# PSUM banks given by expected release in place of a ring, and the engines' orders within a substep arranged anew, in a macaron block (windowed attention, state-space scan, windowed attention)

## The reference, cut to what matters

```python
def attn_layer(x, Wqkv, qs, ksc, Wo):          # 16 heads of 64
    q, k, v = split(x @ Wqkv)                  # x with half of its features shifted by a token
    q = l2norm(q) * qs; k = l2norm(k) * ksc
    q = q * cos * scale + rotate_half(q) * sin * scale
    k = k * cos * inv + rotate_half(k) * sin * inv
    # windows of 32 queries against 64 keys, masked, softmax of 8*q.k, times v
    return local_attention(q, k, v) @ Wo

def ffn_layer(x, g, bln, W1, b1, W2, b2):
    xn = layernorm(x) * g + bln
    a, gate = split(xn @ W1 + b1)              # 341 + 341
    return a * gelu(gate) @ W2 + b2

for i in range(6):
    x = attn_layer(shift_tokens(x), ...) + x
    x = ffn_layer(shift_tokens(x), ...) + x
```

## Time and profile before

| | |
|---|---|
| median of 3 runs | 3372.07 us (3358.28 to 3372.07) |
| the profiled execution's own time | 3364.97 us |
| its span, first to last instruction | 3363.2 us |
| mean granted TensorE clock | 0.946 of full speed |
| VectorE (DVE) busy | 2933.3 us, 87% |
| TensorE (PE) busy | 2891.1 us, 86% |
| GpSimd (POOL) busy | 2423.5 us, 72% |
| ScalarE (ACT) busy | 2059.8 us, 61% |

### The profile page before, as it was taken

One profiled execution on the slowest core, in us unless ns is written; L12 is line 12 of the kernel. 1 busy time (PEld: TensorE's weight loads), 2 busy tenths in 40 slices (PEclk: granted clock), 3 DMA queues, 4 the chain that ended last, 5 costly groups with the idle time before them and its releaser, 6 DMA issues. The chain is left out here.

```text
span 3363.2 us, 132089 instructions
## 1 busy us (share of the span) xinstructions
PE 2891.1 (86%) x57914; PEld 1829.9 (54%) x57914; DVE 2933.3 (87%) x4224; ACT 2059.8 (61%) x3820; POOL 2423.5 (72%) x1679
## 2 busy tenths in 40 slices
PE   5689988988999989897677788999998989998987
PEld 3455555655666655553233455555565555555553
DVE  6789989999999988986898789889899989898984
ACT  3466666666676666665663566666566666566663
POOL 3678787787787787874464678778787787787773
PEclk8899999999999999998897899999999999999998
DMA  5233333333333333320002233333343333342330
GB/s 136 65 80 77 82 91 74 84 92 71 84 92 73 89 85 72 88 65 28 10 4 59 68 81 78 75 93 77 73 101 73 86 90 71 82 94 65 88 74 15
DMA packets 114726, 250.85 MB, mean 75 GB/s; under 512 B 27244, under 2 KB 60648, under 8 KB 114152
## 3 DMA queue, kind: packets, MB, share of 16 engines
q1 hardware_dynamic: 114152, 242.40, 30.5%
HBM read 37.82 MB, written 3.15 MB: 12 GB/s over the span
## 5 line engine op out<-in xcount | busy, mean ns | idle before, releaser
L1096 ACT ACTIVATE squares<-general 128x512 f32<-128x512 f32 x768 | 453.7, 597 | 716.8 <-PE general L661 707.8
L1290 POOL TENSOR_TENSOR probs<-probs,row_sum 128x1024 f32<-128x1024 f32 x192 | 365.4, 1903 | 442.4 <-DVE row_sum L968 442.3
L1270 POOL TENSOR_TENSOR q_ring<-q_ring,partner 128x512 f32<-128x512 f32 x384 | 491.0, 1279 | 203.9 <-DMA partner<-sines 203.3
L881 DVE TENSOR_TENSOR sines<-general,layer_tables 128x512 f32<-128x512 f32 x768 | 515.8, 672 | 85.3 <-ACT squares L1096 81.8
L1270 POOL TENSOR_TENSOR k_ring<-k_ring,partner 128x512 f32<-128x512 f32 x384 | 490.9, 1278 | 0.0
L695 PE MATMUL general<-probs_t,v_buf 32*64 32x64 f32 x24576 | 339.0, 234 | 153.8 <-issue 85.1
L659 PE MATMUL general<-xs_hi,wqkv_lo 128*128 128x512 f32 x768 | 454.2, 591 | 18.5 <-DVE xs_lo L908 8.0
L695 PEld LDWEIGHTS general<-probs_t,v_buf 32*64 32x64 f32 x24576 | 304.0, 134 | 246.1 <-issue 237.5
L1284 POOL TENSOR_TENSOR probs<-probs,q_scale 128x1024 f32<-128x1024 f32 x192 | 365.4, 1903 | 15.1
L722 PE MATMUL general<-k_ring,q_ring 64*32 64x64 f32 (+1 forms) x24576 | 295.3, 223 | 92.5 <-issue 53.1
L671 PE MATMUL general<-att,wo 128*128 128x512 f32 x768 | 366.2, 621 | 4.6 <-ACT att L1166 4.2
(11 more groups left out here) (233 smaller groups left out, 6369.9 us busy)
## 6 DMA issues: line engine op xcount, KB each, us to landing
partner<-sines SPq DMA_DIRECT2D x1536, 128.0 KB, 2.3
wqkv_raw<-in_wqkv SPq DMA_DIRECT2D x80, 208.0 KB, 2.7
wo<-in_wo SPq DMA_DIRECT2D x12, 512.0 KB, 5.1
w<-in_w SPq DMA_DIRECT2D x12, 341.0 KB, 3.2
base_dram<-x SPq DMA_DIRECT2D x8, 256.0 KB, 2.4
att<-in_wqkv SPq DMA_DIRECT2D x2, 1024.0 KB, 6.7
sines<-base_dram SPq DMA_DIRECT2D x8, 256.0 KB, 3.9
w<-in_w SPq DMA_DIRECT2D x12, 128.0 KB
```

The source lines that it names most:

```text
L881: e.tensor_tensor(by_seq(sines[:, i % 2, which, :]), g, both(layer_tables[:, 2 * which + 1, :]), ALU.mult).then_inc(S[f"sin_{side}"], 1)
L1096: e.activation(squares[:, (2 * p + which) % 4, :], general_of(("proj", k, n, p, which))[:, :], ACT.Square).then_inc(S[f"squared_{side}"], 1)
L1270: e.tensor_tensor(y, y, partner[:, i % 2, which, :], ALU.add).then_inc(S[f"rotated_{side}"], 1)
L1290: e.tensor_tensor(y, y, spread_keys(row_sum[:, i % 2, :]), ALU.mult).then_inc(S["probs_done"], 1)
```

## The change

It replaces the ring by a choice: each product takes the bank with the smallest expected release time, `until`, counted in substeps from HOLD; among equals the next in ring order. The walk follows the new order of TensorE. And it moves parts of a substep on TensorE, VectorE and GpSimd. Several names are split (gates and gelus, values_of and hidden and so on), with the same lags as before; on ScalarE the lines change places only among parts that never fall in the same substep, so that its order stays.

```diff
+HOLD = {"proj0": 0.35, "proj1": 0.7, "spread": 0.65, "scores": 0.5, "var": 0.7, "center": 1.1, "gate": 0.6, "value": 0.5, "ffn_out": 0.8, "att": 1, "v": 1, "project0": 1.1, "project1": 1.1}
@@ class Banks
     def around(self, banks):
         self.banks, self.next, self.written = banks, 0, {}
+        self.step, self.until = 0, {}
     def use(self, key, sem, value):
         at = self.next
+        if self.banks == POOL_BANKS:
+            at = min(range(self.banks), key=lambda i: (self.until.get(i, 0), (i - self.next) % self.banks))
         self.next = (at + 1) % self.banks
+        name = f"{key[0]}{key[-1]}" if key[0] in ("proj", "project") else key[0]
+        self.until[at] = self.step + HOLD.get(name, 1)
@@ Banks.stack
-            g = k * ITEMS
+            g, self.step = k * ITEMS, st.t
@@ tensor_stack (Banks.stack in the same order)
                 proj 0, spread
-                if st.out_first:
-                    pe_out(e, w, k, *st.out_first)
                 scores, var
+                if st.out_last is not None:
+                    pe_out(e, w, k, st.out_last, 1)
                 center
+                if st.out_first is not None:
+                    pe_out(e, w, k, st.out_first, 0)
                 ffn_out
-                if st.gates is not None:
-                    pe_gates(e, w, k, st.gates)
                 values_of
-                if st.enter:
-                    pe_enter(e, w, k, *st.enter)
                 proj 1, attention products
-                if st.out_last is not None:
-                    pe_out(e, w, k, st.out_last, 1)
+                if st.gates is not None:
+                    pe_gates(e, w, k, st.gates)
+                if st.enter:
+                    pe_enter(e, w, k, *st.enter)
                 v
@@ vector_stack
                 rotate q, scale the scores, var, last output added
+                if st.first_added is not None:
+                    dve_out(e, w, k, st.first_added, 0)
                 hidden, norms back, first splits
-                if st.split is not None:
-                    dve_split_tokens(e, w, k, st.split)
+                if st.turn:
+                    dve_turn(e, w, k, *st.turn)
                 ffn added
-                if st.out_first:
-                    dve_out(e, w, k, *st.out_first)
                 root, enter
+                if st.split is not None:
+                    dve_split_tokens(e, w, k, st.split)
                 rotate k
-                if st.turn:
-                    dve_turn(e, w, k, *st.turn)
                 norms, sums
-                if st.v:
-                    dve_v(e, w, k, *st.v)
                 sum_inv, max
+                if st.v:
+                    dve_v(e, w, k, *st.v)
@@ gpsimd_stack
                 subtract, scale and affine, scale the scores
-                if st.center is not None:
-                    pool_square(e, w, ("ffn", k, st.center))
                 if st.load_split:
                     pool_split_pair(e, w, k, *st.load_split)
+                if st.enter:
+                    pool_enter(e, w, k, *st.enter)
+                if st.center is not None:
+                    pool_square(e, w, ("ffn", k, st.center))
                 if st.added:
                     pool_rotate(e, w, k, *st.added, 0)
-                if st.exps:
-                    pool_probs(e, w, k, *st.exps)
-                if st.enter:
-                    pool_enter(e, w, k, *st.enter)
                 if st.added:
                     pool_rotate(e, w, k, *st.added, 1)
+                if st.probs:
+                    pool_probs(e, w, k, *st.probs)
```

More of the change, by code:

```diff
@@ L108, in __init__ @@
         self.exps = self.group(t, EXP_LAG)
+        self.probs = self.group(t, PROBS_LAG)
         self.turn = self.group(t, TURN_LAG)
@@ L120, in __init__ @@
         self.spread = self.group(t, SPREAD_LAG)
-        self.out_first = next(((self.item(t, at), i) for i, at in ((0, 17),) if self.item(t, at) is not None), None)
+        self.out_first = self.item(t, 17)
+        self.first_added = self.item(t, 17)
         self.out_last = self.item(t, 21)
+        self.last_added = self.item(t, 21)
+        self.shift = self.item(t, 21)
         self.center = self.item(t, 22)
         self.var = self.item(t, 23)
+        self.var_turn = self.item(t, 23)
         self.root = self.item(t, 24)
         self.gates = self.item(t, 25)
+        self.gelus = self.item(t, 25)
         self.values_of = next(((self.item(t, at), js) for at, js in ((26, (0,)), (27, (1, 2))) if self.item(t, at) is not None), None)
+        self.hidden = next(((self.item(t, at), js) for at, js in ((26, (0,)), (27, (1, 2))) if self.item(t, at) is not None), None)
         self.ffn_out = self.item(t, 28)
+        self.ffn_added = self.item(t, 28)
+        self.ffn_shift = self.item(t, 28)
         self.load = (n // CHUNKS + 1, p) if self.now and n % CHUNKS == CHUNKS - 1 and n // CHUNKS + 1 < DEPTH else None
@@ L287, in stack @@
                 self.var(("ffn", k, st.var))
+            if st.out_last is not None:
+                self.use(("project", k, st.out_last, 1), "att_added", (g + st.out_last) * 2 + 2)
             if st.center is not None:
                 self.norm(("ffn", k, st.center))
+            if st.out_first is not None:
+                self.use(("project", k, st.out_first, 0), "att_added", (g + st.out_first) * 2 + 1)
             if st.ffn_out is not None:
                 self.use(("ffn_out", k, st.ffn_out), "ffn_added", g + st.ffn_out + 1)
-            if st.gates is not None:
-                for j in range(len(HIDDEN_CUTS)):
-                    self.use(("gate", k, st.gates, j), "gelu_done", (g + st.gates) * 3 + j + 1)
             if st.values_of:
@@ L309, in stack @@
                     self.use(("att", k, n, group, j), "att_kept", ((g + n) * GROUPS + group) * 4 + j + 1)
-            if st.out_last is not None:
-                self.use(("project", k, st.out_last, 1), "att_added", (g + st.out_last) * 2 + 2)
+            if st.gates is not None:
+                for j in range(len(HIDDEN_CUTS)):
+                    self.use(("gate", k, st.gates, j), "gelu_done", (g + st.gates) * 3 + j + 1)
+            if st.enter and st.enter[1] == 0:
+                self.norm(("enter", k, st.enter[0]))
+            if st.enter and st.enter[1] == 1:
+                self.var(("enter", k, st.enter[0]))
             if st.v:
@@ L509, in macaron_kernel @@
             for st in PLAN:
-                for key in (("att", k, st.out_last), ("ffn", k, st.ffn_out), ("enter", k, st.enter[0] if st.enter and st.enter[1] == 2 else None)):
+                for key in (("att", k, st.shift), ("ffn", k, st.ffn_shift), ("enter", k, st.enter[0] if st.enter and st.enter[1] == 2 else None)):
                     if key[2] is not None and key[2] not in (range(ITEMS - CHUNKS, ITEMS) if key[0] == "ffn" else ()):
@@ L1194, in scalar_stack @@
                     act_k_inv(e, w, k, *st.spread)
+                if st.split is not None:
+                    act_split_tokens(e, w, k, st.split)
+                if st.center is not None:
+                    act_center(e, w, ("ffn", k, st.center))
                 if st.norms_back is not None:
                     act_norms(e, w, k, st.norms_back)
[L1197 to L1202 removed]
+                if st.gelus is not None:
+                    act_gelus(e, w, k, st.gelus)
                 if st.now:
@@ L1224, in scalar_stack @@
                     act_enter(e, w, k, *st.enter)
-                if st.ffn_out is not None and st.ffn_out < ITEMS - CHUNKS:
-                    n = st.ffn_out
+                if st.ffn_shift is not None and st.ffn_shift < ITEMS - CHUNKS:
+                    n = st.ffn_shift
                     w.wait_ge(S["ffn_added"], k * ITEMS + n + 1)
```

64 lines of the change are left out of this document (27 added, 37 removed).

## The result

The changed kernel takes 3436.53 us (median of four: 3433.2, 3435.01, 3438.04 and a disturbed execution of 4283.97, which the ratio leaves out) against 3371.48: ratio 1.0199, 95% interval 1.0167 to 1.0231. It is slower by 65 us where 3383 was forecast; the time lies inside the range of 3310 to 3440, near its upper end.

The account below looks back on a forecast made before the run. A loop: VectorE bounds p6's second rotation to p2's scores, TensorE p2's attention products to p6's proj 1. Terms 34 + 4 + 9 - 6 - 9 + 10 - 10 - 16 + 2 = +18 us on 3365.0: 3383, range 3310 to 3440.

Parts of the forecast that it names:

- slower by over 0.5%: Case that the kernel takes above 3389 us: both slower rivals and a third of the forecast; chance 0.35.
- the orders of VectorE and GpSimd: GpSimd's second rotation and p1's norms: 0.2 saved per item, -9 us; p5 nothing; inverses +10, waits for v -10.
- p5: Second output projection ahead of proj 1, turn ahead of k's rotation: L915's idle time moves to p6's L881; nothing.
- p1, the gates: Gates go behind proj 1, gelus start about 1 us later, squares of k behind them, covered by VectorE's norms: nothing.
- p2's bank: Substep p2: attention products (L695) wait for value 0's bank (L984) over 30 times, 25 us or more; +34 us.
- p0, p4, p6, the mask: Last att bank one scaling later: p4 +4 us, p0 and p6 nothing; TensorE writes p6's mask, -6 us.
- p7: Proj 1 comes behind p6's v: nothing in the floor item, but the lead for disturbances is gone; +9 us.
- v, sums and inverses: VectorE's even substeps become sum, inverse, max, v: inverse behind its own operand +10 us, waits for v filled -10 us.
- Entries: First items of a stack: the entering chunk's scaling stands earlier, -16 us; the square's hold-up at the entering p2, +2.
- The signs against me: Floor item below 56.5 us, or L933 and L935 losing over 1 us together, would mean the prediction is wrong.
- The clock rival: More bank waits put idle time where the clock falls; ten more low-clock items would be 68 us, 3433; chance 0.07.
- slower for good: p2's full wait paid in every item, 52 us, p4 and p7 another 36, less entries: +72, about 3437; chance 0.15.

Follow-up runs that it names:

- the add alone: Project 0's add put ahead of the norms on VectorE, on top of the kernel before with GpSimd's entering stage first: 3338.18 us, 0.9918 of the kernel before.
- Taking value 0 away by itself: The changed kernel with HOLD of value 0 at 0.6 in place of 0.5: 3401.54 us, 1.015 of the kernel before.
- the gates put back: The changed kernel with the gates and their banks ahead of the values and proj 1 again: 3384.12 us, 1.0076 of the kernel before.
- banks alone: The kernel before with the new bank rule in place of the ring, no order changed: 3383.76 us, 1.0088 of the kernel before.
- orders with the gates back: The changed kernel with the old ring of seven and the gates ahead of the values and proj 1 again: 3371.99 us, 1.0051 of the kernel before.
- the entering stage alone: The kernel before with only GpSimd's entering stage moved ahead of the rotations and probs: 3325.49 us, 0.9914 of the kernel before.
- probs last: The kernel before with GpSimd's entering stage first, plus its second rotation ahead of probs: 3375.72 us, 1.004 of the kernel before.
- all other orders but v: The new orders with gates back, on the ring, and v again between sum and inverse on VectorE: 3372.71 us, 1.0065 of the kernel before.

## Why the prediction was right or wrong

The likeliest case was off: +0.3% forecast, +2.0% measured, in the case "slower by over 0.5%", to which I gave 0.35. The sum was +18 us and the result +65. The forecast's own range ended at 3410; that 3436.53 still lies inside 3310 to 3440 is owed to the room left for the rivals, and not to the terms of the sum. By its steps:

**The step that failed: the orders of VectorE and GpSimd, which I priced one by one,** with "I get 0.2 saved per item" for GpSimd's second rotation and the norms, nothing for p5 and +10 -10 for v: -9 us together. They measured 1.37 points (46 us) together, with the few moves of TensorE that go with them, and the second rotation 1.26 by itself. The port mechanism, a VectorE step that stands until the GpSimd operation under way is done, was as I read it from the earlier trace rows. But I walked GpSimd's new order only past L933 and L935, and never past the variance step in p7, which is short before because a rotation happens to end there. Its median went from 334 to 622 ns. In p1 I was right in sign: L933's median fell from 1105 to 539 ns and L935's rose from 1890 to 2010, 0.45 gained where I had 0.2. That gain gave no time: p1 is shorter, and VectorE waits in p2 instead, as the add alone showed. TensorE sets p2, which was my own reading of the loop, and I did not apply it to this term. The Trainium skill, "SBUF — State Buffer", section "Who interferes with whom", names a tensor_scalar and a cast in a two-port mode and a tensor_tensor with both inputs in SBUF as what contends with GpSimd; L849, L933 and L935 are of these three kinds, though no row tells a two-port mode. By that rule, the trace agrees: the transposes and the operations out of PSUM in p7 kept their length beside the same GpSimd operations (in the same substeps as the two timelines above L847 has 0.70 and 0.71, L886 0.68 in both).

**The second: p1, the gates, "the gelus start about 1 us later and ScalarE squares k behind them, which VectorE's norms (L933 to L938) cover; nothing".** The norms cover nothing of TensorE, whose sums wait for these squares in 39 of the 40 steady items: 14 us over the run. And the gates' three banks are moved with them. Under the ring that alone put 40.7 us of waits on the mask; under the new rule it is what brings value 0 among p2's banks, the next point.

**p2's bank: right in place, and at the edge of count and size.** Forecast: L695 waits for L984 over 30 times, 25 us or more, and 34 us on the period; measured 30 times and 25.1. What it costs on the period isn't shown. Taking value 0 away by itself gave back 0.5 points with overlapping intervals, and TensorE then waited 27 us more for v; with the gates put back it went together with other waits. I had not seen that it hangs on the gates' place.

**p0, p4, p6, the mask: right for the banks, not for p4.** The mask has 319 instructions on ScalarE (320 promised). At p4 the products wait for the scaling 2.5 us in the 40 steady items (4 forecast for the run), and p0 is 0.14 longer in spite of 68.7 us of such waits. But p4 grew by 0.92 an item through waits for which the sum has no term, the ffn's output above all. That the kernel with banks alone is 0.9% slower is not explained.

**p5: right, nothing,** and in the way that was written: L915's idle time fell and L881's rose by as much.

**p7: right in kind.** Proj 1 waits for v 33 times, 21.6 us; without the wait at p2 66 times, 48.8 us.

**v, sums and inverses: nothing net, as forecast, but only beside GpSimd's new order.** VectorE's waits for v did fall (25.2 us in the earlier trace rows), and where v stands turned out to be a matter of ports as well, which I had not considered.

**Entries: right in kind, half in size.** 16 us forecast, 31 in the changed kernel and 29 alone. The wait of L1079 for L1252 fell from 42.5 to 18.8 (under 25 promised), which is 23.7 by itself; I had counted four of its eight waits.

The signs against me: the least disturbed item did not fall below 56.5 but rose to 60.0, for which I had no sign. The clock rival explains at most a part: the mean is 0.942 against 0.946, but the 40 steady items spend 195 us at the lower level against 133 (from the granted clock in the two traces). Items wholly at the upper level take 61.45 us (8 of them) against 59.72 (14), so 1.7 of the 2.5 us an item stand without it. The rival "slower for good" had the time (3437) by another way: it wanted the full wait at p2 in every item, and that wait stayed at 25 us.

**The account.** Gates with value 0's bank +1.23 points (41 us), entries -0.86 (29 to 31 us), the bank rule in these orders +0.25 (1.0076 against 1.0051, not resolved), and the other orders, matched as they are, +1.37 (orders with the gates back, 1.0051, against the entering stage alone, 0.9914). These are steps between neighbouring kernels, so that they add up to +1.99 by construction; each is uncertain by 0.3 to 0.5 points. By themselves p5, the add and v gave +0.15, +0.04 and -0.14, and probs last +1.26. On the way from the entering stage (0.9914) over probs last (1.004) and all other orders but v (1.0065) to v last (1.0051) the loss comes with probs last and stays. But in the kernel with all of them VectorE's busy time is where it was (2935.2 against 2935.1), so the loss has become idle time there. Its waits for the squares at the start of a substep are (L896 is L881; with the entering stage alone 59.8 us, 132 times):

```profile
DVE sines L896 <- ACT squares L1111: 113.8, 181, 2.0
```

30 us of this came with p5, where L915 gave 27 back. What brings the rest when the two engines are matched again stays open; in which substeps it lies is known: with the entering stage alone and then with all the orders p2 takes 8.95 and 9.76, p0 9.54 and 9.76, p1 9.02 and 8.47.

## What to carry to other kernels

When a product is moved in a stream that draws banks in order, two things move: what stands behind its reader on the in-order engine that reads it, and the banks of everything after it; by the waits the second was the larger here under both rules. Short VectorE steps between SBUF tiles in a kernel that keeps GpSimd busy are a hidden coupling of the two streams: before either stream is reordered, list each such step with the GpSimd operation that it ends with (not every kind is held: the 128 x 16 reciprocal never was), and judge both orders as a pair. A trace answers for its own execution only: where two kernels differ by less than a kernel's executions do among themselves, look first whether the two profiled ones show the difference at all. A change that bundles a gain with losses is worth taking apart: one moved call of it is 0.9% faster than the kernel before.

## What the runs showed of the hardware that I had not expected

A 128 x 16 step on VectorE (L849) takes 181 ns at the least and up to 1935 ns with a GpSimd operation under way (the kernel with the second rotation ahead of probs), ten times its length, and where it takes over 300 ns it ends 33 to 49 ns behind that operation (43 to 50 of its 56 times in every one of the fourteen traces). A 128 x 16 reciprocal right behind it was never held (255 to 261 ns). The profile books this as busy time, so no row of idle time shows it. VectorE's total of busy time at an unchanged count of instructions (2918 to 3016 us over these kernels, 4224 each time) is the quickest sign of it, but not of the time lost: with all the orders it was back at 2935.2 us and the kernel still at 1.0051.

Waits for a bank can be many and next to free: in the profiled execution the new bank rule alone put 92 waits with 147 us on TensorE, most of them in its spare time, and left the mean item as long as it was. That kernel's 0.9% over all its executions stays unexplained.
